# One transposition, one copy and two transfers for the negative maxima of two column groups instead of one

## The reference

```python
x = x + tanh(g_xattn[0]) * xattn(layernorm(x), ctx, ctx)     # 32 query heads, 8 key/value heads, head width 16
x = x + tanh(g_ffn[0]) * ffn(layernorm(x), Wr, Wg, Wu, Wd, Wsg, Wsu, Wsd, Wse)
# xattn, for each batch b:
scores = einsum('bkgsd,bktd->bkgst', qh, kh) / sqrt(16)
weights = softmax(scores, axis=-1)          # over the 128 keys t
out = einsum('bkgst,bktd->bkgsd', weights, vh)
```

## Time and profile before

| What | Value |
|---|---|
| Median of three runs | 2383.96 us |
| Profiled execution: span from the first to the last instruction | 2381.9 us |
| Mean granted TensorE clock, as a share of 2.4 GHz | 0.984 |
| TensorE matmul (PE) busy | 2290.9 us, 96% |
| VectorE (DVE) busy | 1144.9 us, 48% |
| ScalarE (ACT) busy | 815.7 us, 34% |
| GpSimd (POOL) busy | 589.5 us, 25% |
| Attention stage | from 0 to about 712 us |

### The profile page before, as it was taken

One profiled execution on the slowest core, in us unless ns is written; L12 is line 12 of the kernel. 1 busy time (PEld: TensorE's weight loads), 2 busy tenths in 40 slices (PEclk: granted clock), 3 DMA queues, 4 the chain that ended last, 5 costly groups with the idle time before them and its releaser, 6 DMA issues.

```text
span 2381.9 us, 41762 instructions
## 1 busy us (share of the span) xinstructions
PE 2290.9 (96%) x12545; PEld 1775.2 (75%) x12545; DVE 1144.9 (48%) x2214; ACT 815.7 (34%) x1426; POOL 589.5 (25%) x1378
## 2 busy tenths in 40 slices
PE   7999999999991699999999999999999999999998
PEld 5777777777771577777777777777777777777776
DVE  6999999999987422322323223232332223323232
ACT  6888888888883110101101011010110101101010
POOL 5666666666657100000000000000000000000000
PEclk9999999999995899999999999999999999999999
DMA  2444444444445422222222212322123221232211
GB/s 77 138 133 136 134 133 136 131 138 131 137 121 192 100 78 87 93 87 72 77 98 95 85 62 77 111 89 77 62 77 114 86 77 62 88 103 86 77 44 42
DMA packets 238538, 234.83 MB, mean 99 GB/s; under 512 B 88625, under 2 KB 164401, under 8 KB 238514
## 3 DMA queue, kind: packets, MB, share of 16 engines
q1 hardware_dynamic: 234162, 221.89, 29.8%
q0 software_dynamic: 4352, 12.65, 1.7%
HBM read 161.88 MB, written 71.57 MB: 98 GB/s over the span
## 4 chain that ended last, share of the span: by engine, by line
PE 66%; DVE 0%; DVEq 0%; issue 0%
PE acc L1053 7%; PE p_g L1066 7%; PE p_g L1068 7%; PE p_g L1067 7%; PE acc L1054 7%; PE acc L1055 7%; PE p_u L1068 7%; PE p_u L1067 7%; PE p_u L1066 7%; PE p_x L1096 2%; PE p_y L1083 2%; PE p_x L1083 2%; PE p_x L1074 0%; PE p_y L1089 0%; DVE keys L1036 0%; DVEq L848 0%
## 5 line engine op out<-in xcount | busy, mean ns | idle before, releaser
L997 DVE TENSOR_TENSOR act_f<-p_u,act_f 128x512 f32<-128x512 f32 x176 | 121.7, 691 | 1035.3 <-PE p_u L1068 1035.3
L968 ACT ACTIVATE act_f<-p_g 128x512 f32<-128x512 f32 x176 | 105.2, 598 | 1203.2 <-PE p_g L1068 1203.2
L530 DVE TENSOR_REDUCE negmax<-p_max 128x8 f32<-128x1024 f32 x256 | 313.1, 1223 | 66.5 <-PE p_max L672 52.0
L1053 PE MATMUL acc<-wd_h,hh 128*128 128x512 f32 x704 | 279.1, 396 | 0.0
L1066 PE MATMUL p_g<-xh,wgu_h 128*128 128x512 f32 x704 | 276.3, 392 | 1.3 <-PEq L721 1.3
L1068 PE MATMUL p_g<-xh,wgu_l 128*128 128x512 f32 x704 | 274.5, 390 | 0.0
L1067 PE MATMUL p_g<-xl,wgu_h 128*128 128x512 f32 x704 | 274.5, 390 | 0.0
L1054 PE MATMUL acc<-wd_l,hh 128*128 128x512 f32 x704 | 274.3, 390 | 0.0
L1055 PE MATMUL acc<-wd_h,hl 128*128 128x512 f32 x704 | 274.2, 390 | 0.0
L1068 PE MATMUL p_u<-xh,wgu_l 128*128 128x512 f32 x704 | 273.9, 389 | 0.0
L1067 PE MATMUL p_u<-xl,wgu_h 128*128 128x512 f32 x704 | 273.9, 389 | 0.0
(11 more groups left out here) (141 smaller groups left out, 3705.2 us busy)
## 6 DMA issues: line engine op xcount, KB each, us to landing
ew<-in_L_ffn_Wg_dram SPq DMA_DIRECT2D x32, 704.0 KB
ew<-in_L_ffn_Wu_dram SPq DMA_DIRECT2D x32, 704.0 KB
xs<-in_x_dram SPq DMA_DIRECT2D x64, 256.0 KB, 2.6
xres<-in_x_dram SPq DMA_DIRECT2D x64, 256.0 KB, 2.8
out_dram<-x SPq DMA_DIRECT2D x64, 256.0 KB, 2.0
xn_rows<-xn SPq DMA_DIRECT2D x64, 256.0 KB, 3.0
xn_cols<-xnT SPq DMA_DIRECT2D x64, 256.0 KB, 2.4
chosen<-xn_cols SPq DMA_DIRECT2D x16, 1024.0 KB, 5.6
```

What stands on the lines that cost most here:

```text
L530: nc.vector.tensor_reduce(negmax[c % 2][:, :].rearrange("p (g i) -> p i g", i=G), p_max[:, :, :].rearrange("p a (h g t) -> p (a h) g t", g ...
L1053: mm(acc[:, j, :], a[:, t], wd_h[:, f, :], start=(f == 0), stop=False)
```

## The change

`negmax` grows to 128x16 and `mt` to 16x128. Group c of a batch writes 8 columns of the tile of its half h = c // 2, in the order key/value head, group, query head. Only slots 0 and 2 still carry the last step of each engine: at slot 2 of B the half h = 0 (groups 0 and 1 of B), at slot 0 of B+1 the half h = 1 (groups 2 and 3 of B). One transposition (128x16), one copy (16x128) and two DMAs serve a half; each DMA lays eight rows of 128 into 1024 adjacent elements of one partition, those of two groups. TensorE waits for a half ahead of `p_exp` in slots 0 and 2, for both groups of it.

```diff
-            negmax = [sb(f"negmax{i}", [128, 8]) for i in range(2)]
-            mt = [sb(f"mt{i}", [8, 128], F32R) for i in range(2)]
+            negmax = [sb(f"negmax{i}", [128, 16]) for i in range(2)]
+            mt = [sb(f"mt{i}", [16, 128], F32R) for i in range(2)]
...
-            p_mt = ps("p_mt", [8, 128])
+            p_mt = ps("p_mt", [16, 128])
@@ SyncE
-                        m = (B - 1, 3) if c == 0 else (B, c - 1)
-                        if m[0].ok:
-                            b, cc = m
-                            wait(sp, mt_done, 4 * b.n + cc + 1)
+                        b, h = (B - 1, 1) if c == 0 else (B, 0)
+                        if c % 2 == 0 and b.ok:
+                            wait(sp, mt_done, 2 * b.n + h + 1)
                             for g2 in range(2):
-                                sp.dma_start(qt[b.par][64 * g2:64 * g2 + 1, cc, :].bitcast(F32),
-                                             mt[cc % 2][4 * g2:4 * g2 + 4, :].bitcast(F32)).then_inc(mrow_in[cc % 2], 16)
+                                sp.dma_start(qt[b.par][64 * g2:64 * g2 + 1, 2 * h:2 * h + 2, :].rearrange("p c n -> p (c n)").bitcast(F32),
+                                             mt[h][8 * g2:8 * g2 + 8, :].bitcast(F32)).then_inc(mrow_in[h], 16)
@@ ScalarE
-                        b, cc = (B - 1, 3) if c == 0 else (B, c - 1)
-                        if b.ok:
-                            act.wait_ge(mt_mm, 4 * b.n + cc + 1)
-                            wait(act, mrow_in[cc % 2], 32 * (2 * b.n + cc // 2))
-                            nc.scalar.activation(mt[cc % 2][:, :], p_mt[:, :], ACT.Copy).then_inc(mt_done, 1)
+                        b, h = (B - 1, 1) if c == 0 else (B, 0)
+                        if c % 2 == 0 and b.ok:
+                            act.wait_ge(mt_mm, 2 * b.n + h + 1)
+                            wait(act, mrow_in[h], 32 * b.n)
+                            nc.scalar.activation(mt[h][:, :], p_mt[:, :], ACT.Copy).then_inc(mt_done, 1)
@@ VectorE
-                            wait(dve, mt_mm, 4 * B.n + c - 1)
-                            nc.vector.tensor_reduce(negmax[c % 2][:, :].rearrange("p (g i) -> p i g", i=G),
+                            if c % 2 == 0:
+                                wait(dve, mt_mm, 2 * (B.n - 1) + c // 2 + 1)
+                            nc.vector.tensor_reduce(negmax[c // 2][:, :].rearrange("p (g c i) -> p c i g", g=2, c=2)[:, c % 2, :, :],
@@ TensorE
-                            pe.wait_ge(mrow_in[c % 2], 32 * (2 * b.n + c // 2 + 1))
+                            if c % 2 == 0:
+                                pe.wait_ge(mrow_in[c // 2], 32 * (b.n + 1))
...
-                        b, cc = (B - 1, 3) if c == 0 else (B, c - 1)
-                        if b.ok:
-                            pe.wait_ge(max_done, 4 * b.n + cc + 1)
-                            wait(pe, mt_done, 4 * b.n + cc)
-                            last = tr(p_mt[:, :], negmax[cc % 2][:, :], ident[:, :])
+                        b, h = (B - 1, 1) if c == 0 else (B, 0)
+                        if c % 2 == 0 and b.ok:
+                            pe.wait_ge(max_done, 4 * b.n + 2 * h + 2)
+                            wait(pe, mt_done, 2 * b.n + h)
+                            last = tr(p_mt[:, :], negmax[h][:, :], ident[:, :])
                             last.then_inc(mt_mm, 1)
```

## The result

| | Before | After |
|---|---|---|
| Median | 2383.94 us | 2491.98 us |
| Span of the profiled execution | 2381.9 us | 2491.1 us |
| Period of a batch in the attention stage | 10.88 us | 12.57 us (mean of two) |

The ratio is 1.0448, with a 95% interval of 1.0430 to 1.0466: 108 us slower, where 69 were forecast. From the start of the last `p_exp` to the end it is 1668 us before and 1669 us after, so the loss lies in the attention.

The account below looks back on a forecast made before the run. TensorE was taken to bound the attention stage. Two windows growing 0.55 us each gave 1.10 us a batch over 64 batches, 69 us after the early batches; span 2451 us, median 2453 us, range 2422 to 2500.

Parts of the forecast that it names:

- TensorE sets the pace, and the rows have 5.92 us: Attention stage before: TensorE busy for all 10.88 us of a period; maxima have 5.92 us from transposition to use.
- The new wait in slots 0 and 2: TensorE idles ahead of `p_exp`: 2.94 us needed where 2.39 pass, so 0.55 us more per window, twice a batch.
- The saved transpositions: Two fewer a batch on TensorE, 0.11 us each; inside the waiting windows, so worth nothing.
- 2.94 us for the chain: Transposition start to `p_exp`: copy done 0.58, SyncE 0.03, first issue 0.65, landing 1.60, signal and weight load 0.08; range 2.7 to 3.5.
- Issue and landing unchanged with eight rows: SyncE's DMAs of the maxima: eight source rows instead of four leave issue (0.65 us) and landing (1.60 us) unchanged.
- With TensorE held up, ScalarE catches up.: Copy of the maxima on ScalarE: 0.58 us from transposition start to copy end taken for both halves, despite slot 0's later start.
- The fixed cost of about 2.0 us: Skill's DMA cost whatever the size, measured on another issue path; used for landing, it made the chain 3.34 us.
- the 2504 us: Time worked out with the skill's 2.0 us as the landing: 2453 + 128 x 0.40.
- The first rival: Rows of maxima still land in time at `p_exp`, so only the transpositions count: 2370 us; chance 4%.
- The range: Whole kernel's time, 2422 to 2500 us, leaving out the first two rivals and the third's dear end.
- step 4: Start of the second DMA issue to its landing: 1.6 us, range 1.35 to 2.2; 1.4 to 2.0 for the forecast's bounds.

Follow-up runs that it names:

- The doubled transposition: Kernel before, with each of its 256 transpositions of the maxima issued twice into the same tile: 2416.84 us, ratio 1.0129.
- the joined DMA in the kernel before: Kernel before, with the two DMAs of a group joined into one that writes two partitions: 2383.64 us, ratio 0.9999.
- The waits alone: Kernel before, with TensorE waiting in slots 0 and 2 for both groups' maxima, not in slots 1 and 3; nothing merged: 2477.44 us, ratio 1.0391.
- the merged work without the wait: Kernel after, with the maxima landing in a tile nobody reads and TensorE not waiting for them: 2375.14 us, ratio 0.9962.
- the kernel with the earlier transposition: Kernel after, with the maxima's transposition and copy moved ahead of those of the queries within the slot: 2388.59 us, ratio 1.0024.
- The joined DMA: Kernel after, with the two DMAs of a half joined into one that writes two partitions: 2395.11 us, ratio 1.0043.

## Why the prediction was right, and where it was off

- *TensorE sets the pace, and the rows have 5.92 us.* Right. The doubled transposition shows the first: what is added to TensorE is paid in full. That the rows had slack is shown by the joined DMA in the kernel before (no change).
- *The new wait in slots 0 and 2.* Right in mechanism, place and releaser. The waits alone cost 93 us with nothing merged, and the merged work without the wait costs nothing.
- *The saved transpositions lie inside the windows and are worth nothing there.* Right: they become worth something (9 us) only where the wait is gone. Their size, 0.11 us, holds for an addition and was too high for a removal (0.07).
- *2.94 us for the chain.* This is the term that was mis-sized; 3.21 us were measured. By its steps, read from the starts and ends in the traces, means over 100 to 800 us of the kernel with the waits alone (four rows a transfer, nothing merged, 113 windows) and of the kernel after (eight rows, 112 windows):

| Step, us | Forecast | Waits alone | After |
|---|---|---|---|
| To the start of the copy | 0.31 | 0.33 | 0.37 |
| The copy | 0.27 | 0.27 | 0.27 |
| To the first issue | 0.03 | 0.06 | 0.02 |
| First to second issue | 0.65 | 0.66 | 0.72 |
| Start of the second issue to `p_exp` | 1.60 + 0.08 | 1.79 | 1.83 |
| Sum | 2.94 | 3.10 | 3.21 |

The difference of 0.27 us, 128 times, is 35 of the 39 us that the forecast missed.

- *Issue and landing unchanged with eight rows.* This was wrong by the smaller part. Of the 0.27 us, 0.16 are there with four rows and nothing merged, and that kernel lies 24 us above 2453. The eight rows can answer for 0.06 us of issue and 0.04 of landing. The step that was most too short is the last one. The packets were through 1.38 us after the start of the second issue, 1.32 or 1.33 with four rows (1.34 was read for the kernel before; there the issue began at 406.93, not 406.89, which gives 1.30); what follows the last packet took 0.46 us in both, where the sum had 0.34.
- *"With TensorE held up, ScalarE catches up."* The copy starts 0.31 or 0.39 us after the transposition, 0.37 in the mean. The copy of the queries ahead of it isn't all of the reason: in the kernel with the earlier transposition ScalarE is idle, and the copy still starts 0.39 us after (TensorE, then ScalarE). Why it is sometimes 0.31 and sometimes 0.39 stays open.

```profile
406.90 0.27 PE L674 MATMUL p_mt<-ident,negmax 128*16 128x128 f32 x1
```

```profile
407.29 0.27 ACT L434 ACTIVATE mt<-p_mt 16x128 fp32r<-16x128 f32 x1 [0.57 <-PE p_mt L674]
```

- *The fixed cost of about 2.0 us* that the Trainium skill gives ("DMA: Bandwidth & Descriptors", section "Anatomy of one DMA — SWDGE (gpsimd) path"). From the start of the issue to the use the trace has 1.83 us; the sum had 1.68, and with the skill's figure it would have had 2.08. So the sum's term was the nearer one. That the 2504 us worked out with it missed by 12 us, where the forecast missed by 39, is luck: a term too long made up for others too short. A transfer of 4 KB whose packets take 0.15 us supports the section's main point, that the time is not in the data.
- *The first rival* named the point from which it decides: a chain of 2.28 us. The joined DMA comes within 0.2 us of it (2.46) and loses 11 us; with about 0.9 us more window the loss is gone. Both sides of that point have thus been seen.
- *The range* came from step 4 alone. It held, but near its end, because the misses of three steps all went one way.

## What to carry to other kernels

Merging small steps of a pipeline saves their cost once, but it makes the first part wait for the last and the last be needed as early as the first: count how many slots lie between production and use before and after, and hold the whole chain (copy, issue, landing, signal) against it. If the chain doesn't fit, look at the order before dropping the merge: moving the step within its slot brought back 103 of 108 us, with the same instructions. And ask how much the merge can give at best: here 9 us of 2384, against a wait that is paid 128 times.

## What the runs showed of the hardware

- One DMA that writes two partitions 64 apart occupied the issuing queue for 0.53 us, from 8 rows as from 16; a DMA of one partition took 0.58 us from four rows and 0.64 from eight (medians). So for these shapes the issue time went mainly with the number of DMAs.
- From the start of its issue, a DMA with eight source rows of 512 bytes was usable after 1.79 to 1.89 us (mean 1.83, kernel after), one with four rows after 1.70 to 1.91 us (mean 1.79, waits alone). Packets were through after 1.38 and after 1.32 or 1.33 us, and 0.46 us followed the last packet in both.
- An added transposition cost 0.11 us, a removed one gave 0.07.
